# Moving the two subtractions of the bf16 split from GpSimd to VectorE in a two-layer graph network kernel

## The reference, cut to what matters

```python
w_m = (efeat @ W_msg + b_msg).reshape(E, in_f, -1)      # E x 16 x 16
w_a = (efeat @ W_attn + b_attn).reshape(E, in_f, -1)
h_src = feat[src][:, :, None]
e1 = w_m * h_src
e2 = w_a * h_src
seg_max = jax.ops.segment_max(e2, dst, num_segments=N)
ex = jnp.exp(e2 - seg_max[dst])
denom = jax.ops.segment_sum(ex, dst, num_segments=N)
attn = ex / denom[dst]
ft = jax.ops.segment_sum(e1 * attn, dst, num_segments=N)
return ft.sum(axis=1)
```

## Time and profile before

| | |
|---|---|
| median of 3 runs | 7086.64 us (7085.68 to 7087.65) |
| span of the profiled execution | 7092.7 us (no other time of that execution is given) |
| GpSimd busy | 5238.8 us, 74% of the span |
| VectorE busy | 3819.3 us, 54% |
| TensorE matmul busy | 2890.4 us, 41% |
| ScalarE busy | 1322.9 us, 19% |
| layer 1, VectorE's part in 40 slices | 6 to 9 tenths busy |
| layer 1, GpSimd's part in 40 slices | 6 to 8 tenths busy, 4 in the last |
| L311 gathers, layer 1 | 1746, 2465.9 us |
| L361 and L365, GpSimd | 53 each, 90.3 and 90.0 us |

### The profile page before, as it was taken

One profiled execution on the slowest core, in us unless ns is written; L12 is line 12 of the kernel. 1 busy time (PEld: TensorE's weight loads), 2 busy tenths in 40 slices (PEclk: granted clock), 3 DMA queues, 4 the chain that ended last, 5 costly groups with the idle time before them and its releaser, 6 DMA issues. The chain is left out here.

```text
span 7092.7 us, 58394 instructions
## 1 busy us (share of the span) xinstructions
PE 2890.4 (41%) x13892; PEld 2119.0 (30%) x13893; DVE 3819.3 (54%) x4819; ACT 1322.9 (19%) x1283; POOL 5238.8 (74%) x3977
## 2 busy tenths in 40 slices
PE   3520000000000000000167777777777777777777
PEld 1100000000000000000045555555555565555555
DVE  8211111111111111113168888898989989888887
ACT  3520000000000000000022222222223222222222
POOL 0336778878888888886768887888887778788774
PEclk9999999999999999999778888888788888878888
DMA  5870111111111011111100101001010111111110
GB/s 171 275 212 6 6 6 6 6 6 6 6 6 6 6 6 6 6 6 7 10 9 9 9 9 11 9 9 12 9 12 9 12 12 9 11 12 12 11 11 7
DMA packets 156805, 172.85 MB, mean 24 GB/s; under 512 B 125700, under 2 KB 144341, under 8 KB 150279
## 3 DMA queue, kind: packets, MB, share of 16 engines
q0 software_dynamic: 137888, 62.56, 9.9%
q1 hardware_dynamic: 18865, 110.05, 4.8%
q10 hardware_dynamic: 32, 0.01, 0.0%
HBM read 72.66 MB, written 108.58 MB: 26 GB/s over the span
## 5 line engine op out<-in xcount | busy, mean ns | idle before, releaser
L311 POOL DMA_INDIRECT gath<-h_dram,hidx x1746 | 2465.9, 1412 | 540.6 <-issue 540.6
L311 POOL DMA_INDIRECT gath<-table,blkidx x1746 | 2135.4, 1223 | 537.3 <-issue 534.8
L469 PE MATMUL psT<-identb,stage 125*100 125x125 bf16 x2544 | 234.5, 272 | 3032.2 <-POOL stage L365 3019.9
L658 DVE TENSOR_TENSOR work<-gath 125x768 f32<-125x768 f32 x52 | 49.8, 958 | 2029.6 <-DMA gath<-table,blkidx 2029.6
L469 PEld LDWEIGHTS psT<-identb,stage 125*100 125x100 bf16 x2544 | 218.6, 170 | 3052.5 <-POOL stage L365 2908.0
L486 PE MATMUL psS<-stage,ident 125*125 125x256 f32 x3492 | 1020.4, 452 | 249.7 <-DVE stage L1080 248.9
L486 PEld LDWEIGHTS psS<-stage,ident 125*125 125x125 f32 x3492 | 757.4, 224 | 446.7 <-DVE stage L1080 309.5
L481 PE MATMUL psS<-arena,ident 125*125 125x256 f32 x3492 | 866.0, 386 | 1.0 <-issue 1.0
L475 PE MATMUL psW<-wst,stage 100*125 100x256 bf16 x3492 | 621.9, 301 | 474.1 <-DVE stage L1030 244.9
L1030 DVE TENSOR_TENSOR arena<-psW,gath 125x768 f32 (+1 forms) x582 | 535.0, 950 | 264.8 <-DMA gath<-h_dram,hidx 172.9
L481 PEld LDWEIGHTS psS<-arena,ident 125*125 125x125 f32 x3492 | 623.6, 191 | 74.6 <-issue 1.2
(11 more groups left out here) (214 smaller groups left out, 2762.4 us busy)
## 6 DMA issues: line engine op xcount, KB each, us to landing
table<-arena SPq DMA_DIRECT2D x50, 1610.0 KB
gath<-table,blkidx POOLq DMA_INDIRECT x1746, 2.6
gath<-h_dram,hidx POOLq DMA_INDIRECT x1746
efp<-in_edge_attr SPq DMA_DIRECT2D x1, 12890.6 KB, 46.9
table<-arena SPq DMA_DIRECT2D x50, 186.9 KB
arena<-first_dram POOLq DMA_DIRECT2D x1, 915.5 KB, 11.8
info<-info_dram POOLq DMA_DIRECT2D x2, 439.5 KB, 14.1
blkidx<-pairp,bst POOLq DMA_INDIRECT x53, 2.8
```

The costliest lines, as they stand in the source:

```text
L311: pool.indirect_dma_start(out=gath[:, q, s, :], out_offset=None, in_=rows, in_offset=bass.IndirectOffsetOnAxis(ap=idx[:, q, s:s + 1].bitca ...
L469: last = nc.tensor.transpose(psTb[0:KE, t % 3, j, 0:PN], efs[:, 8 * t + j, :], identb[0:PN, 0:PN])
```

## The change

The two subtractions become VectorE instructions with the same operands, semaphores and waits. GpSimd's stream keeps only the DMAs. The first pair, for window 0, stands before VectorE's loop. In window k, `residue(k + 1)` stands behind the first maximum L1042 and before `edge_valid(k + 1)`, and `last_part(k + 1)` behind L1054 and before `finish`. The waits of `edge_block` are as they were.

```diff
@@ GpSimd @@
-            def residue(w):
-                pool.wait_ge(m["hi_done"], w + 1)
-                nc.gpsimd.tensor_tensor(efres, efin, efs[:, :, HI:HI + D], ALU.subtract).then_inc(m["res_done"], 1)
-
-            def last_part(w):
-                pool.wait_ge(m["mid_done"], w + 1)
-                nc.gpsimd.tensor_tensor(efs[:, :, LO:LO + D], efres, efs[:, :, MID:MID + D], ALU.subtract).then_inc(m["lo_done"], 1)
...
-                    residue(k)
                     edge_block(k + 1, 1 - q)
                     for b in range(MINH):
                         gather(h2_d, hidx, q, b, HALF, hgath)
-                        if b == MINH // 2 - 1:
-                            last_part(k)
...
-            residue(2 * pairs)
-            last_part(2 * pairs)
@@ VectorE @@
+            def residue(w):
+                dve.wait_ge(m["hi_done"], w + 1)
+                V.tensor_tensor(efres, efin, efs[:, :, HI:HI + D], ALU.subtract).then_inc(m["res_done"], 1)
+
+            def last_part(w):
+                dve.wait_ge(m["mid_done"], w + 1)
+                V.tensor_tensor(efs[:, :, LO:LO + D], efres, efs[:, :, MID:MID + D], ALU.subtract).then_inc(m["lo_done"], 1)
+
             edge_ids(0, 0)
+            residue(0)
+            last_part(0)
             edge_valid(0, 0)
...
                     scores(0)
                     scores(1)
                     V.tensor_tensor(macc, score[:, q, 0:BLK, :], score[:, q, BLK:2 * BLK, :], ALU.max)
+                    residue(k + 1)
                     edge_valid(k + 1, 1 - q)
...
                     V.tensor_tensor(diff[:, q, :], mold, mnew[:, q, :], ALU.subtract).then_inc(m["d_ready"], 1)
-
+                    last_part(k + 1)
```

## The result

The changed kernel takes 7262.62 us (median of 4 runs, 7255.35 to 7266.14) against 7086.16 us before: a ratio of 1.0248, 95% interval 1.0233 to 1.0262, some 176 us slower. The prediction was 7189 us, in the range 7108 to 7268.

A forecast was written before the change was run, and what follows sets the result against it. In the last stage GpSimd's stream was taken as the bound, by little, with VectorE in step. Six stretches gave +96 us, the last stretch, head and last window +2 each: +102 on the 7086.64 us median, 7189 us, range 7108 to 7268.

The forecast's parts named there:

- the step that decides: At each window's head, GpSimd's next gathers wait for VectorE's `residue`, so the engines take turns: +96 us over six stretches.
- Release to L347: GpSimd's time from the end of `residue` to its first edge load: 1.0 us a step.
- L347 to first gather: GpSimd's time from the first edge load to the first gather of the set: 3.03 us a step.
- Last gather to first score: Time from the end of GpSimd's last gather to VectorE's first score: 2.33 us a step.
- First score to the end of the maximum: VectorE's first two score blocks and L1042 at a window's head, after a wait for gathers: 7.5 us a step.
- the collisions that go: Gathers beside L1042 and behind L365 no longer held up: 1.8 us less a step.
- the tie: `edge_block(k+1)` on GpSimd waits for `residue(k)`, now on VectorE behind the scores that need the previous set of gathers.
- "dearer" rival: No collision goes (+85 us), or GpSimd needs 2 us more after a long wait: 7275 us, chance 0.15.
- The transposes: TensorE's transposes wait for `last_part` but fit by 0.2 us: no cost; without cover, 1 to 2 us in VectorE-bound windows.
- the step rule: Each stretch of windows becomes gather time plus 0.30 us per gather plus 12.7 us per step.
- the head: The stage's start: first set ready 4 us sooner, three binding steps at about 2 us each, +2 us in all.
- The faster rival: GpSimd is freed, nothing new binds and VectorE bounds every window: -58 us, 7029 us, chance 0.10.

The follow-up runs named there:

- the last experiment: The changed kernel with `last_part` cut to one of the 48 slots in windows 1 to 51: 7234.39 us, ratio 1.0189 to the kernel before.

## Why the prediction was right, and where it was short

**Order.** It named the step that decides, the alternation, and its terms read off the traces of before came out one by one. The number itself held by little: 7263 us is 5 us inside the upper end of the range, and the loss was 176 us where 102 were forecast. Release to L347: 1.0 predicted, 0.96 on average over 44 steps. L347 to first gather: 3.03 and 3.03. Last gather to first score: 2.33 and 2.21. First score to the end of the maximum: 7.5 and 7.39 on average, 7.96 in half of the windows and 6.0 to 7.7 in the others. `residue` and `last_part`: 0.96 and 0.95. VectorE's wait for gathers: 250 to 350 us in over 40 windows, 323 in 45. L1046's mean: 1.76 and 1.758; L1019's: 0.45 and 0.431.

**The mis-sized term** is the collisions that go, 1.8 us a step. From window 4 to 48 the gathers' busy time fell from 2108 to 2088 us, 0.46 us a step. This is 44 x 1.34 = 59 us, and the miss in these stretches is 150.6 - 95.5 = 55 us. The other terms nearly cancel: the gaps between gathers are 0.31 us instead of 0.30, which adds 11 us, and the measured terms of the list above came out 14 us shorter in all. The tenth gather, behind L365, did become shorter, by 0.6 us on average. The first one did so in 15 of the 44 windows, those that are like the window shown: there it lay beside L1042, in one beside an L1046, and took 2.1 to 2.8 us, and takes 1.6 to 1.75 now. In the other 29 it had taken 1.2 us and takes 1.6 to 1.75 now, beside an L1044: the tie puts the start of each set at the same place in VectorE's scores, and there it meets a new collision in every window. `last_part` costs 0.6 to 0.8 us a window by the last experiment. The prediction had a price of that size for it, from the row of 2.72 us, against the 0 that follows from the inference in the Trainium skill's "SBUF — State Buffer", "Who interferes with whom", and left it within the bounds instead of in the sum. Its "dearer" rival, no collision goes, was nearer than its forecast.

**The transposes** were said to cost nothing, because `finish` covers them. In window 0 there is no `finish`. VectorE in the trace after:

```profile
3559.45 1.76 DVE L1078 TENSOR_TENSOR stage<-stage,arena  x1 [5.05 <-ACT arena L609]
```

That is 5 us of the +22 in the first stretch; the cover was checked in the window shown and not in the first. In all later windows it held: VectorE's waits of this kind are 5.5 us in the whole stage. The other three steps of that stretch grew by 5.3 to 5.8 us each where I had 2: I had put a round number there and not the step rule. With the 4.4 us gained ahead of it the head lost 17.6 us where 2 were forecast, which is the second part of the miss.

**The faster rival**, 7029 us, did not come about for the change and is nevertheless near what was measured with `residue` ahead of the wait or the tie cut: 7003 and 7030 us. The estimate of what VectorE alone would need was good to 26 us and to 1 us; the order kept the change from it.

**Two readings** of the prediction don't hold as they stand. It puts L1046 and L1019 under one rule, for VectorE instructions with two SBUF inputs, but L1019 is a tensor_scalar with one tensor input and two values per partition; its 2.29 us beside L361 are measured, and by which rule it is held up was not tried. And "for its whole length" fits L1046 only roughly: it began 0.78 us ahead of L365 and took 2.34 us more than alone, beside an L365 of 1.70 us. Neither bears on the step that decides.

**The median** moved by 176.5 us and the profiled span by 171.8: putting the difference of spans on the median was good to 5 us.

## What to carry to other kernels

Before an instruction moves from one engine's stream to another's, list what waits for its semaphore, and ask where in the new stream it stands relative to the waits there: a producer that the other engine needs early must not stand behind a wait for that engine's own last product, or the two engines take turns. Its length is of little account (36 of 176 us here), its place decides (890 us between the best and the worst of four). Where a stream is shortened and the kernel gets slower, move the instruction within its new stream before taking the move back; and when collisions are counted as saved, count those that the moved instruction and the new start of the transfers make.

## What the hardware showed that I had not expected

- TensorE's mean granted clock was 0.917 in the profile before and 0.678 in the one after, and 0.906 in another run of the changed kernel, which took 7262.73 us against the 7262.51 and 7266.14 us of runs at 0.678. The low clock lies in the first 19 of 40 slices, most of it the first layer, of which TensorE is at work in the first three slices alone; from window 4 on the stretches show 0.82 to 0.87 before and 0.84 to 0.85 after. The mean clock of a run said nothing of its time.
- After a stand of TensorE of 5.48 us six matmuls took 2.77 us instead of 1.46, at a granted clock of 0.50 (1.2 GHz, the lower of its two levels) in the 3.4 us behind the stand, where it had been 1.00 ahead of it. VectorE's fourth half block then came 2.21 us late. Over the 44 steps the first scores took 7.39 us instead of the 6.02 without a wait, so a wait of VectorE for DMA costs more than its own length.
- The same indirect DMA takes GpSimd 1.2 us to issue alone and up to 2.7 us beside a VectorE tensor_tensor with two SBUF inputs. What counts is whether it starts while the other runs. In layer 1 of the changed kernel 760 gathers start inside an L1068, L1078, L1044 or L1000, more than 0.2 us before its end, and every one ends 1.05 to 1.09 us behind it, wherever in it the gather started. The 415 that start inside an L1027, which has one input in PSUM, take 1.18 to 1.22 us, like one alone. So the price of a collision is what is left of the VectorE instruction, and shifting the start of a set changes it. The gathers' mean in layer 1 was 1354 ns with no L1044 beside the gathers, 1381 with a short `last_part` and 1400 in the changed kernel.
